# Routed experts: results scattered to two token tables and summed on the matmul engine, instead of gathered after the last unit

## The chip, the cores and the metric

The kernel runs on one core of one Trainium2 chip. The metric is device time in microseconds (us) of one execution. TensorE (PE) does matmuls into the eight PSUM banks, VectorE (DVE), ScalarE (ACT) and GpSimd (POOL) do elementwise work, SyncE (SP) issues plain DMAs, and POOL issues the indirect DMAs, whose rows are addressed by an index per partition.

## The reference

Four layers on 1024 tokens of width 256: a linear attention, a gated attention, a decay attention and a grouped attention with experts, each followed by `x = layernorm(x + layer(x))`. Only the end of the last layer matters here. A router picks two of eight experts for each token, and its two probabilities weigh the results:

```python
topv, topi = jax.lax.top_k(xt @ gate_w, 2);  probs = softmax(topv)
for e in range(8):
    h = silu(xt @ w1[e]) * (xt @ w3[e])
    out = out + w[:, e:e + 1] * (h @ w2[e])      # w: probs at the two picked experts, else 0
x = layernorm(x + h_attn + out)
```

## The kernel before

Tokens lie as 8 tiles of 128 (`NT` = 8). `layer1_experts` starts after the grouped attention. Every fp32 matrix of the experts is split in a high part (rounded to the matmul's fp32r) and a low part (the rest), and a product is three matmuls (`split_product`, L125).

**Routing.** The second half of the norm (`norm.apply`, L589 on DVE and L623 on ACT) writes `c.scratch`, PE turns it (L648) and multiplies it with the router's weights, and DVE works out for each token its two *slots*: the tokens of one expert get consecutive rows of a table in DRAM, each expert starting at a multiple of 128. `TILES` = 23 units of 128 slots always suffice, and all 23 are computed, empty ones too. `scratch_l`, the low part of `c.scratch`, is made in two halves, the first on POOL (L2103), the second on DVE (L2169).

**Getting the rows to their units.** POOL scatters each of the 8 token tiles twice (16 indirect DMAs, L2108) to `slot_rows` in DRAM, which SP had filled with zeros long before. Units 0 to 3 don't wait for this: PE gathers their rows with one-hot matmuls (L2426). When the 16 scatters have landed SP loads the rows of units 4 and 5, then the weights of expert 3, then the rows of units 6 to 9, 10 to 15 and 16 to 22 (L2079). PE turns a unit's rows (`turn`, L2434) in the order that is written out by hand; `turn(4)` is the first that needs the scatters, `turn(6)` the first that needs the second load.

**A unit.** `up` (two projections, 24 matmuls in all with their products), SiLU on ACT, `gate` on DVE, `turn_hidden` (L2459), high and low parts, `down` (12 matmuls to one half of PSUM bank 7), then DVE copies the result to `rows[:, j]` (`leave`, L2237) and SP stores it to `slot_outs`, row by row as the slots lie (L2093). `down(j)` waits until `leave(j - 1)` is done.

**Weights.** SP loads an expert's three matrices (1536 KB) to one of two stages. Experts 0 and 1 are split by ACT and DVE, experts 2 to 7 by POOL: three high parts (L2122), then three low parts (L2126), then `w_ready`. Of each ring of three experts POOL waits until the units of the expert it overwrites are done.

**The end.** POOL waits until all 23 stores have landed and gathers with 16 indirect DMAs (L2131, for each token tile the rows of its first and of its second slot). For each token tile, as it lands, DVE adds both rows with their probabilities to `c.y` (L2298, twice), takes the moments (L2301, L2304, L2306), ACT the root (L2387), DVE the reciprocal and the shift (L2308, L2309), ACT applies them (L2390) and SP stores the tile.

Of the kernel before, what the change touches and what calls it, by code (L numbers as in the profile page):

```python
# [53 lines left out]
class Core:  # L54


    def __init__(self, nc, dram, out, ctx):
# [17 lines left out]
        self.scratch = self.tile(ctx, "scratch", [P, NT, D])  # L75

        self.slot_rows = nc.dram_tensor("slot_rows", (SLOTS, D), F32).ap()
# [583 lines left out]
def layer0_gated_attention(c, norm, following, next_norm, later_norm):  # L661
# [10 lines left out]
    with ExitStack() as ctx:  # L672
# [22 lines left out]
        z_ready, picked_ps, kv_ready, nm_ready, pT_ready, rs_ready, o_scaled, chain = c.sems(  # L695
# [3 lines left out]
        c.finished += pe_sems  # L699
# [488 lines left out]
def layer1_decay_attention(c, norm, pre, following, next_norm):  # L1188
# [7 lines left out]
    with ExitStack() as ctx:  # L1196
# [24 lines left out]
        TURN_AT = PAIRS + 12  # L1221
        SECOND_AT = 1
# [52 lines left out]
        def _(dve):  # L1275
# [31 lines left out]
            for s in range(STEPS + 1):  # L1307
# [21 lines left out]
                if 6 <= s < 14:  # L1329
                    following.split(dve, s - 6)  # L1330
                if s == PAIRS + 3:
                    scale(0)
                    dve.wait_ge(acc_out, 2)
# [214 lines left out]
def layer1_grouped_attention(c, norm, pre, next_norm, router):  # L1548
# [7 lines left out]
    with ExitStack() as ctx:  # L1556
# [54 lines left out]
        def _(sp):  # L1611
# [18 lines left out]
            zeros = c.warm16[:].bitcast(F32).unsqueeze(1).broadcast_to((P, SLOTS // P, D))  # L1630
            sp.dma_start(c.slot_rows.rearrange("(n p) d -> p n d", p=P), zeros).then_inc(c.rows_zeroed, 16)
# [329 lines left out]
class RoutedExperts:  # L1961
# [4 lines left out]
    def __init__(self, c, ctx, router):  # L1966
        self.c, self.router = c, router
        self.rows, self.rows_zeroed = c.slot_rows, c.rows_zeroed
        self.outs = c.nc.dram_tensor("slot_outs", (SLOTS, D), F32).ap()
# [4 lines left out]
def layer1_experts(c, norm, pre):  # L1974
# [8 lines left out]
    GATHERS = 8  # L1983
# [3 lines left out]
    X0, T_BANK, Y_BANK = 5, 4, 7  # L1987
    with ExitStack() as ctx:
# [19 lines left out]
        slot_max = sb("slot_max", [P, NT])  # L2008
# [16 lines left out]
        rows = sb("rows", [P, TILES, D])  # L2025
# [9 lines left out]
        back = [c.xT[:].rearrange("p k (a d) -> p (k a) d", d=D), c.scratch[:]]  # L2035
# [9 lines left out]
        back_in = c.sems(ctx, "f", " ".join(f"back_in{n}" for n in range(GATHERS)))  # L2045
        scattered, outs_in, stored, hot_made = c.cleared_sems("scattered outs_in stored hot_made")
# [9 lines left out]
        def rows_landed(eng, j):  # L2056
            n = next(n for n, (first, last) in enumerate(chunks) if j < last)
            eng.wait_ge(rows_in[n], 16)
# [10 lines left out]
        def _(sp):  # L2069
            def load_weights(e):  # L2070
                if e in (2, 3):
                    sp.wait_ge(w_low, e - 1)
                if e >= 2:
                    sp.wait_ge(w_ready, e - 1)
                sp.dma_start(stage[e % 2][:], c.dram["w_experts"][e]).then_inc(stage_in[e % 2], 16)
# [24 lines left out]
        def _(pool):  # L2100
            pool.wait_ge(norm.shift_ready, norm.so["shift_ready"] + 2)
            pool.wait_ge(s_high, 1)
            pool.tensor_tensor(scratch_l[:, 0:4, :], c.scratch[:, 0:4, :], scratch_h[:, 0:4, :].bitcast(F32), ALU.subtract).then_inc(s_low, 1)  # L2103
            pool.wait_ge(pre.rows_zeroed, 16)
            pool.wait_ge(slots_ready, 1)
            for t in range(NT):
                for k in range(2):
                    pool.indirect_dma_start(pre.rows, bass.IndirectOffsetOnAxis(slots[:, k, t:t + 1].bitcast(mybir.dt.uint32), 0), c.scratch[:, t, :], None).then_inc(scattered, 16)  # L2108
            pool.wait_ge(table_ready, 1)
            for e in range(2, EXPERTS):  # L2110
# [6 lines left out]
                pool.wait_ge(w_ready, e)  # L2117
                pool.wait_ge(stage_in[e % 2], 16 * (e // 2 + 1))
                at = e % RING * WC
                for n in range(3):  # L2120
                    cols = slice(at + PARTS[n].start, at + PARTS[n].stop)
                    pool.tensor_copy(wh[:, cols], stage[e % 2][:, PARTS[n]]).then_inc(pool_high, 1)  # L2122
                for n in range(3):
                    cols = slice(at + PARTS[n].start, at + PARTS[n].stop)
                    pool.wait_ge(pool_high, 3 * (e - 2) + n + 1)
                    low = pool.tensor_tensor(wl[:, cols], stage[e % 2][:, PARTS[n]], wh[:, cols].bitcast(F32), ALU.subtract)  # L2126
                low.then_inc(w_ready, 1)
            pool.wait_ge(outs_in, 16 * TILES)
            for t in range(NT):
                for k in range(2):  # L2130
                    pool.indirect_dma_start(back[k][:, t, :], None, pre.outs, bass.IndirectOffsetOnAxis(slots[:, k, t:t + 1].bitcast(mybir.dt.uint32), 0)).then_inc(back_in[t * GATHERS // NT], 16)  # L2131

        @block.vector
        def _(dve):
# [32 lines left out]
            weight_low(0, 0)  # L2167
            dve.wait_ge(s_high, 2)
            dve.tensor_tensor(scratch_l[:, 4:NT, :], c.scratch[:, 4:NT, :], scratch_h[:, 4:NT, :].bitcast(F32), ALU.subtract).then_inc(s_low, 1)  # L2169
# [28 lines left out]
            dve.tensor_copy(slots[:], slot_f[:]).then_inc(slots_ready, 1)  # L2198
            dve.tensor_tensor(slot_max[:], slot_f[:, 0], slot_f[:, 1], ALU.max)
# [9 lines left out]
            link(dve.tensor_tensor(slot_diff[:], slot_min[:], slot_max[:], ALU.subtract))  # L2209
            link(dve.tensor_tensor(slot_in[:], from_half[:], slot_diff[:].unsqueeze(2).broadcast_to((P, NT, 2)), ALU.mult))  # L2210
            link(dve.tensor_tensor(slot_in[:], slot_in[:], slot_max[:].unsqueeze(2).broadcast_to((P, NT, 2)), ALU.add))
# [23 lines left out]
            def leave(j):  # L2235
                dve.wait_ge(y_ps, j + 1)
                dve.tensor_copy(rows[:, j, :], ps[:, Y_BANK, j % 2 * D:(j % 2 + 1) * D]).then_inc(y_out, 1)  # L2237
# [39 lines left out]
            for j in range(5, TILES):  # L2277
                gate(j)
                hidden_low(j - 1)
                if j + 2 < TILES:  # L2280
                    row_low(j + 2)
                if j >= 6:
# [5 lines left out]
            leave(TILES - 1)  # L2288

            dve.wait_ge(p_ready, 1)  # L2290
            per = NT // GATHERS
            for g in range(GATHERS):
# [335 lines left out]
```

## Time and profile before

| | |
|---|---|
| three runs | 965.43 us median (965.05 to 967.98) |
| profiled execution | 968.8 us, span of its instructions 967.0 us |
| granted TensorE clock, mean | 0.977 |
| PE busy | 894.3 us, 92% |
| DVE, POOL, ACT busy | 654.6, 455.8, 416.8 us |
| grouped attention ends, experts begin | about 789 us into the span |
| last matmul ends | 937.4 us |

The page divides the span into 40 slices. PE is at nine tenths or more in nearly all of them up to the last, in which it is at 0 and its granted clock at 0.5: nothing is multiplied from 937.4 us on. The chain of waits, which is followed back from the last instruction, shows what fills that end.

### The profile page before, as it was taken

What the parts mean: (1) busy time and instruction counts of PE and PEld (TensorE: products, weight loads), DVE (VectorE), ACT (ScalarE), POOL (GpSimd) and SP (SyncE); (2) the same over time, 40 slices, a digit from 0 to 9 for tenths busy, and PEclk for the clock granted to TensorE, in tenths of its full rate; (3) what the DMA queues carried; (4) which work ended last, traced back from release to release, by engine and by line L of the source; (5) the groups of instructions that cost most, each with busy time, mean ns of one, the idle gap of its engine ahead of it and who ended that gap; (6) DMA issues with size and microseconds to landing.
All of it is one profiled execution on the core that took longest, in us unless ns stands there. A gap on an engine that the chain in (4) does not pass through costs nothing. (4 is left out here: it accounts for less than half of the span.)

```text
span 967.0 us, 17722 instructions
## 1 busy us (share of the span) xinstructions
PE 894.3 (92%) x6526; PEld 731.5 (76%) x6536; DVE 654.6 (68%) x1154; ACT 416.8 (43%) x1002; POOL 455.8 (47%) x409
## 2 busy tenths in 40 slices
PE   9998999988999999999999879999999978899970
PEld 5566666767888888888888668888888955788860
DVE  3577678975566675576665689778888758476436
ACT  4323456643544545445455345434232444233322
POOL 2000400015667766776766255554545414888405
PEclk9999999999999999999999899999999999999995
DMA  5000200004433433333332101131000031664014
GB/s 194 1 2 2 66 1 2 2 19 122 150 110 101 124 109 105 89 105 119 104 109 62 55 12 50 45 103 40 1 2 1 1 126 37 240 242 137 28 41 124
DMA packets 53459, 72.05 MB, mean 75 GB/s; under 512 B 4992, under 2 KB 45056, under 8 KB 52224
## 3 DMA queue, kind: packets, MB, share of 16 engines
q1 hardware_dynamic: 51840, 66.72, 21.8%
q0 software_dynamic: 1536, 4.20, 1.4%
q8 instruction: 55, 0.90, 0.4%
q14 instruction: 28, 0.23, 0.1%
HBM read 61.73 MB, written 9.18 MB: 73 GB/s over the span
## 5 line engine op out<-in xcount | busy, mean ns | idle before, releaser
L1765 ACT ACTIVATE e_probs<-ps,e_neg_max 128x256 f32<-128x256 f32 (+1 forms) x128 | 52.1, 419 | 121.9 <-DVE e_neg_max L1691 121.9
L125 PE MATMUL ps<-xTl,d_wh 128*128 128x512 f32 x192 | 80.8, 421 | 2.8 <-DVE d_s_m L1281 2.8
L1281 DVE TENSOR_TENSOR d_s_m<-ps,d_decay 128x768 f32<-128x768 f32 x64 | 58.3, 952 | 34.4 <-PE ps L1443 32.1
L1644 POOL TENSOR_TENSOR e_q_T<-xT 128x512 f32<-128x512 f32 x32 | 41.1, 1284 | 82.0 <-DVE xT L1679 82.0
L1086 POOL TENSOR_TENSOR d_wh<-d_stage,d_nought 128x512 fp32r<-128x512 f32 x32 | 43.2, 1351 | 75.8 <-PE ps L125 33.1
L125 PE MATMUL ps<-xTh,d_wh 128*128 128x512 f32 x192 | 76.3, 397 | 0.0
L125 PE MATMUL ps<-xTh,d_wl 128*128 128x512 f32 x192 | 76.1, 396 | 0.0
L615 POOL TENSOR_TENSOR n_rstd<-n_var,half_power 128x4 f32<-128x4 f32 x6 | 6.1, 1023 | 133.5 <-DVE n_var L561 133.4
L1360 ACT ACTIVATE d_gated_hi<-d_gated 128x512 fp32r<-128x512 f32 x32 | 20.2, 632 | 108.6 <-DVE d_gated L1287 108.6
L125 PE MATMUL ps<-f_wl,wh_gated 128*128 (+2 forms) x184 | 65.2, 354 | 1.9 <-DVE f_rows L2237 0.7
L125 PE MATMUL ps<-f_wh,wh_gated 128*128 (+2 forms) x184 | 62.8, 341 | 0.0
L125 PE MATMUL ps<-f_wh,wl_gated 128*128 (+2 forms) x184 | 62.6, 340 | 0.0
L868 ACT ACTIVATE g_probs<-ps,g_neg_max 128x256 f32<-128x256 f32 (+1 forms) x128 | 43.2, 422 | 31.6 <-DVE g_neg_max L786 31.1
L1157 DVE TENSOR_TENSOR wl_gated<-d_q_T,wh_gated 128x512 fp32r<-128x512 f32 x32 | 22.7, 710 | 50.0 <-ACT wh_gated L1142 50.0
L1650 POOL TENSOR_TENSOR e_probs<-e_probs,e_rsum 128x256 f32<-128x256 f32 x64 | 52.5, 841 | 6.8 <-DVE e_rsum L1696 6.8
L1094 POOL TENSOR_TENSOR d_wh<-d_stage,d_nought 128x256 fp32r<-128x256 f32 x32 | 26.9, 839 | 48.2 <-PE ps L125 48.0
L1272 POOL TENSOR_TENSOR d_sq_sum<-d_sq_sum,d_sq 128x512 f32<-128x512 f32 x32 | 44.2, 1382 | 10.6 <-ACT d_sq L1364 10.6
L125 PEld LDWEIGHTS ps<-xTl,d_wh 128*128 128x128 f32 x192 | 36.4, 190 | 15.7 <-issue 8.8
L1088 POOL TENSOR_TENSOR d_wl<-d_stage,d_wh 128x512 fp32r<-128x512 f32 x32 | 43.3, 1352 | 2.5
L2126 POOL TENSOR_TENSOR f_wl<-f_stage,f_wh 128x1024 fp32r<-128x1024 f32 x18 | 43.3, 2435 | 0.0
L125 PEld LDWEIGHTS ps<-xTh,d_wh 128*128 128x128 f32 x192 | 36.4, 189 | 9.0
L125 PEld LDWEIGHTS ps<-xTh,d_wl 128*128 128x128 f32 x192 | 36.5, 190 | 7.1
(389 smaller groups left out, 2894.3 us busy)
## 6 DMA issues: line engine op xcount, KB each, us to landing
d_decay<-in_decay SPq DMA_DIRECT2D x32, 384.0 KB, 3.8
f_stage<-in_w_experts SPq DMA_DIRECT2D x8, 1536.0 KB, 7.1
d_stage<-in_w_decay SPq DMA_DIRECT2D x32, 256.0 KB, 3.0
d_stage<-in_w_decay SPq DMA_DIRECT2D x32, 128.5 KB, 3.4
d_stage_v<-in_w_decay SPq DMA_DIRECT2D x32, 128.0 KB, 2.3
d_stage<-in_w_decay SPq DMA_DIRECT2D x32, 128.0 KB, 2.4
slot_rows<-warm SPq DMA_DIRECT2D x1, 2944.0 KB, 10.5
slot_outs<-f_rows SPq DMA_DIRECT2D x23, 128.0 KB, 3.2
```

Of the source, the lines that this page charges most:

```text
L125: mm = pe.matmul(out, w(k), x(k), start=(opens and n == 0), stop=(closes and n == 3 * len(ks) - 1))
L868: ex = act.activation(probs[:, n % KEPT, i, cols], ps[:, banks(n) + i, cols], ACT.Exp, bias=neg_max[:, n % 4, t, i:i + 1])
L1086: pool.tensor_tensor(wh, qk, self.nought[:].unsqueeze(1).broadcast_to((P, KD, 2 * P)), ALU.add).then_inc(self.qk_high, 1)
L1088: pool.tensor_tensor(wl, qk, wh.bitcast(F32), ALU.subtract).then_inc(self.qk_split, 1)
L1094: pool.tensor_tensor(wh, g, self.nought[:].unsqueeze(1).broadcast_to((P, KD, P)), ALU.add).then_inc(self.g_high, 1)
L1157: dve.tensor_tensor(self.q_lo, self.q_T[:], self.q_hi.bitcast(F32), ALU.subtract).then_inc(self.qk_lo, 1)
L1272: pool.tensor_tensor(sq_sum[:, cols], sq_sum[:, cols], sq[:], ALU.add).then_inc(sq_added, 1)
L1281: dve.tensor_tensor(s_m[:, s % 2, 2 * b:2 * b + 2, :], ps[:, 2 + 2 * b:4 + 2 * b, 0:CAUSAL], decay[:], ALU.mult).then_inc(sm_ready, 1)
L1644: pool.tensor_tensor(dst, by_cos[:, n % 2, :], by_sin[:, n % 2, :], ALU.add).then_inc(roped, 1)
L1650: mul = pool.tensor_tensor(part, part, rsum[:, s % 4, t, :].unsqueeze(2).broadcast_to((P, 2, cols.stop - cols.start)), ALU.mult)
L1765: ex = act.activation(probs[:, s % KEPT, i, cols], ps[:, 2 + i, cols], ACT.Exp, bias=neg_max[:, s % 4, t, i:i + 1], accum_out=sums[:, s % ...
L2126: low = pool.tensor_tensor(wl[:, cols], stage[e % 2][:, PARTS[n]], wh[:, cols].bitcast(F32), ALU.subtract)
```

## The change

- `slot_rows` gets two columns more (1032 bytes a row): the token's number and its larger slot, scattered along with the row. The table is filled beforehand with zeros, 2048 + partition, and -1. Units 0 to 3 get these two columns by a DMA of their own, ahead of the row loads of units 6 on.
- From them DVE works out, during units 13 to 16, where each slot's result belongs: row `token` of a first table if the slot is the smaller of its token, row `1024 + token` of a second if it is the larger, and a spare row if the slot is empty.
- POOL scatters each unit's result there (`unit_out`, 23 indirect DMAs), all of them behind its last weights. The 23 plain stores of SP and the 16 gathers are gone.
- SP loads the first table (four DMAs of two token tiles) when units 0 to 21 have landed, and the second when the last has.
- PE sums in PSUM: identity times `c.y`, then diagonal matrices of the probabilities times the first and the second table, all fp32. DVE builds the 16 diagonals behind the last unit's copy. DVE and ACT read the sums from PSUM, in pairs of token tiles, with the factors of a pair behind the moments of the next.
- POOL splits an expert's up weights first (`w_ready`), its down weights last (`w_low`); `down` waits for the latter.
- The first half of `scratch_l` moves from POOL to DVE.

```diff
+        self.scratch_rows = self.tile(ctx, "scratch", [P, NT, D + 2])
+        self.scratch, self.tokens, self.slot_max = self.scratch_rows[:, :, 0:D], self.scratch_rows[:, :, D], self.scratch_rows[:, :, D + 1]
+        self.slot_rows = nc.dram_tensor("slot_rows", (SLOTS, D + 2), F32).ap()
...
+            sp.dma_start(rows[:, 0:GATHERED, D:D + 2], pre.rows[0:GATHERED * TILE, D:D + 2].rearrange("(n p) d -> p n d", p=P)).then_inc(rows_in[1], 16)
             for n in range(1, len(chunks)):
                 load_rows(n)
-            for j in range(TILES):
-                if 4 <= j < EXPERTS:
-                    load_weights(j)
-                sp.wait_ge(y_out, j + 1)
-                sp.dma_start(pre.outs[j * TILE:(j + 1) * TILE, :], rows[:, j, :]).then_inc(outs_in, 16)
+            for e in range(4, EXPERTS):
+                load_weights(e)
+            sp.wait_ge(outs_in, 16 * (TILES - 1))
+            for g in range(PAIRED):
+                load_back(0, 2 * g, 2).then_inc(first_in[g], 16)
+            sp.wait_ge(last_in, 16)
+            for g in range(PAIRED):
+                load_back(1, 2 * g, 2).then_inc(back_in[g], 16)
...
-            pool.wait_ge(norm.shift_ready, norm.so["shift_ready"] + 2)
-            pool.wait_ge(s_high, 1)
-            pool.tensor_tensor(scratch_l[:, 0:4, :], c.scratch[:, 0:4, :], scratch_h[:, 0:4, :].bitcast(F32), ALU.subtract).then_inc(s_low, 1)
...
+            def unit_out(j):
+                pool.wait_ge(dest_ready, 1)
+                pool.wait_ge(y_out, j + 1)
+                pool.indirect_dma_start(pre.outs, bass.IndirectOffsetOnAxis(dest[:, j:j + 1].bitcast(mybir.dt.uint32), 0), rows[:, j, 0:D], None).then_inc(
+                    outs_in if j < TILES - 1 else last_in, 16)
...
+                high(0)
+                high(1)
+                low(0)
+                low(1).then_inc(w_ready, 1)
+                high(2)
+                low(2).then_inc(w_low, 1)
+            for j in range(TILES):
+                unit_out(j)
...
+            for k in range(2):
+                for t in range(NT):
+                    dve.tensor_scalar(scaling[:, k, t, :], c.ident, p_of[:, k, t:t + 1], None, ALU.mult).then_inc(scaled, 1)
...
+            for g in range(PAIRED):
+                moments(g)
+                if g >= 1:
+                    factors(g - 1)
+            factors(PAIRED - 1)
...
             turn_hidden(TILES - 1)
-            down(TILES - 2, at[TILES - 2][1])
-            down(TILES - 1, at[TILES - 1][1])
+            down(TILES - 2, *at[TILES - 2])
+            for t in (2, 3):
+                added(t, c.ident, c.y[:, t, :], first=True)
+            down(TILES - 1, *at[TILES - 1])
+            for t in (0, 1, 4, 5, 6, 7):
+                added(t, c.ident, c.y[:, t, :], first=True)
+            keep_warm(c, pe, ps[:, X0, :], 12)
+            for g in range(PAIRED):
+                pe.wait_ge(scaled, 2 * g + 2)
+                pe.wait_ge(first_in[g], 16)
+                ... two matmuls, scaling[:, 0, t, :] by back[0][:, t, :]
+            for g in range(PAIRED):
+                pe.wait_ge(back_in[g], 16)
+                for t in (2 * g, 2 * g + 1):
+                    mm = added(t, scaling[:, 1, t, :], back[1][:, t, :])
+                mm.then_inc(summed, 1)
```

## Rows read from the trace of the kernel before

**Rows 1.** Chain of waits from 834 us on: start us, us, what.
```profile
834.77 2.38 DMA slot_rows<-scratch,f_slots
837.17 2.76 DMA f_rows<-slot_rows
...
935.01 0.44 DVE f_rows L2237
...
935.68 1.70 PE ps L125 x12
937.41 0.43 DVE f_rows L2237
...
939.53 0.26 issue
...
964.29 0.60 ACT x L2390
```

**Rows 2.** Groups from 937 us on: busy us, mean ns of one | idle before.
```profile
L2131 POOL DMA_INDIRECT xT<-slot_outs,f_slots x8 | 7.8, 978 | 37.5 <-DMA slot_outs<-f_rows 35.4 <-issue 2.1
L2131 POOL DMA_INDIRECT scratch<-slot_outs,f_slots x8 | 7.7, 958 | 2.4 <-issue 2.4
```

**Rows 3.** Timeline, POOL: start us, us, instruction [idle before].
```profile
808.49 1.27 POOL L2108 DMA_INDIRECT slot_rows<-scratch,f_slots  x1 [14.10 <-DVE f_slots L2198]
810.07 2.85 POOL L2108 DMA_INDIRECT slot_rows<-scratch,f_slots  x1 [0.31 <-issue]
...
897.28 7.10 POOL L2126 TENSOR_TENSOR f_wl<-f_stage,f_wh 128x1024 fp32r<-128x1024 f32 x3
```

**Rows 4.** Timeline, 960.3 to 961.9 us: moments and factors of one token tile.
```profile
960.39 0.43 DVE L2301 BATCH_NORM_STATS2 f_stats<-y 128x6 f32<-128x256 f32 x1
...
961.26 0.20 ACT L2387 ACTIVATE f_sd<-f_var 128x1 f32<-128x1 f32 x1 [1.36 <-DVE f_var L2306]
961.49 0.16 DVE L2308 RECIPROCAL f_rstd<-f_sd 128x1 f32<-128x1 f32 x1 [0.27 <-ACT f_sd L2387]
961.69 0.16 DVE L2309 SCALAR_TENSOR_TENSOR f_shift<-f_mv,f_rstd 128x1 f32<-128x1 f32 x1
```

**Rows 5.** Groups by shape: busy us, mean ns of one | idle before.
```profile
L465 PE MATMUL ps<-a_wo,a_o_nT 128*128 128x256 f32 x32 | 8.0, 392 | 0.1
L2349 ACT ACTIVATE wh_gated<-ps,r_wcol 128x256 fp32r<-128x256 f32 x4 | 1.7, 470 | 8.9 <-PE ps L2426 8.9
L591 DVE TENSOR_SCALAR scratch<-y,n_mv,n_comb 128x256 f32<-128x256 f32 x6 | 2.1, 402 | 0.0
```

**Rows 6.** Timeline, 788 to 802 us: the second half of the norm and the router.
```profile
788.92 1.41 DVE L547 BATCH_NORM_STATS2 n_stats<-y 128x6 f32<-128x256 f32 x4 [0.32 <-PEq L1556]
...
791.84 2.70 DVE L589 TENSOR_SCALAR scratch<-y,n_rstd 128x256 f32<-128x256 f32 x2
791.96 0.91 ACT L623 ACTIVATE scratch<-y,n_rstd 128x256 f32<-128x256 f32 x2 [0.53 <-DVE n_shift L583]
792.00 2.39 POOL L2103 TENSOR_TENSOR f_wl<-scratch,f_wh 128x1024 fp32r<-128x1024 f32 x1 [14.07 <-DVE n_shift L583]
...
794.59 1.10 PE L648 MATMUL ps<-consts,scratch 128*128 128x128 f32 x8 [1.80 <-DVE scratch L589]
...
798.67 1.22 DVE L2169 TENSOR_TENSOR f_wl<-scratch,f_wh 128x1024 fp32r<-128x1024 f32 x1
...
801.40 0.23 DVE L2171 COPY f_lg<-ps 128x64 f32<-128x64 f32 x1 [1.51 <-PE ps L2407]
```

**Rows 7.** Timeline, SP and PE, around the row loads (the last SP row covers three issues).
```profile
837.64 0.42 SPq L2075 DMA_DIRECT2D f_stage<-in_w_experts  x1
838.11 3.84 SPq L2079 DMA_DIRECT2D f_rows<-slot_rows  x3
...
846.22 0.38 PE L2434 MATMUL ps<-consts,f_rows 128*128 128x128 f32 x2
```

**Rows 8.** DMA issues: KB each, us from issue to landing.
```profile
f_rows<-slot_rows SPq DMA_DIRECT2D x1, 512.0 KB, 7.9
```

More of the change, by code:

```diff
@@ L1987, in layer1_experts @@
     X0, T_BANK, Y_BANK = 5, 4, 7
+    DEST_AT = 13
     with ExitStack() as ctx:
@@ L2024, in layer1_experts @@
         wl = sb("wl", [P, RING * WC], F32R)
-        rows = sb("rows", [P, TILES, D])
+        rows = sb("rows", [P, TILES, D + 2])
+        spare_picked, spare_used = picked[:].rearrange("p a t e -> p (a t e)"), used[:].rearrange("p e n -> p (e n)")
+        slot_id, second, empty, dest_f = (spare_picked[:, n * TILES:(n + 1) * TILES] for n in range(4))
+        dest = sb("dest", [P, TILES], mybir.dt.int32)
+        order = spare_used[:, 0:2 * NT].rearrange("p (a t) -> p a t", a=2)
+        shares = spare_used[:, 2 * NT:6 * NT].rearrange("p (a t) -> p a t", a=4)
+        p_of = sb("p_of", [P, 2, NT])
         rows_hot = [w[:].rearrange("p k (a s) -> p (k a) s", s=WINDOW) for w in (c.xTh, c.xTl)]
@@ L2165, in weight_low @@
                 return dve.tensor_tensor(wl[:, cols], stage[e][:, PARTS[part]], wh[:, cols].bitcast(F32), ALU.subtract)
-            weight_low(0, 0)
-            dve.wait_ge(s_high, 2)
-            dve.tensor_tensor(scratch_l[:, 4:NT, :], c.scratch[:, 4:NT, :], scratch_h[:, 4:NT, :].bitcast(F32), ALU.subtract).then_inc(s_low, 1)
+            for half in range(2):
+                four = slice(4 * half, 4 * half + 4)
+                dve.wait_ge(s_high, half + 1)
+                dve.tensor_tensor(scratch_l[:, four, :], c.scratch[:, four, :], scratch_h[:, four, :].bitcast(F32), ALU.subtract).then_inc(s_low, 1)
+                if half == 0:
+                    weight_low(0, 0)
             dve.wait_ge(lg_ps, 1)
@@ L2460, in turn_hidden, with down @@
                 mm.then_inc(hid_ps, 1)
-            def down(j, at):
+            def down(j, ready, at):
+                pe.wait_ge(w_low, ready)
                 pe.wait_ge(lo_ready, j + 1)
-                if j < 2:
-                    pe.wait_ge(w_low, j + 1)
                 need(pe, y_out, j)
@@ L2493, in _ @@
             turn(5)
-            down(3, at[3][1])
+            down(3, *at[3])
             up_next(4)
@@ L2502, in _, with added @@
                 if j >= 6:
-                    down(j - 2, at[j - 2][1])
+                    down(j - 2, *at[j - 2])
+            def added(t, factor, tile, first=False):
+                return pe.matmul(ps[:, t // 2, t % 2 * D:(t % 2 + 1) * D], factor, tile, start=first and t % 2 == 0, stop=not first, skip_group_check=True)
             turn_hidden(TILES - 1)
-            down(TILES - 2, at[TILES - 2][1])
-            down(TILES - 1, at[TILES - 1][1])
+            down(TILES - 2, *at[TILES - 2])
[8 more added lines that the diff above has]
+                pe.wait_ge(first_in[g], 16)
+                for t in (2 * g, 2 * g + 1):
+                    pe.matmul(ps[:, g, t % 2 * D:(t % 2 + 1) * D], scaling[:, 0, t, :], back[0][:, t, :], start=False, stop=False, skip_group_check=True)
+            pe.wait_ge(scaled, 2 * NT)
+            for g in range(PAIRED):
+                pe.wait_ge(back_in[g], 16)
+                for t in (2 * g, 2 * g + 1):
+                    mm = added(t, scaling[:, 1, t, :], back[1][:, t, :])
+                mm.then_inc(summed, 1)
 def build(nc, dram, out):
```

138 lines of the change are left out of this document (86 added, 52 removed).

## Prediction

> **What bounds the kernel now.** I read the slices of the page first: TensorE is full until the last slice and idle in that one. Then the chain of waits. It is one unbroken run of matmuls through units 4 to 22, so in that stretch only work on PE, or a wait that PE gets, changes the time; what DVE, ACT and POOL do beside it is free as long as they keep up. The chain leaves PE at 937.38 us and goes copy, store, POOL, load, DVE, ACT, final store [rows 1]. The last copy ends at 937.41 + 0.43 = 937.84 us and the span at 967.0: a tail of 29.2 us. The groups of that stretch name its owner: POOL's 16 gathers of 0.96 to 0.98 us with 0.30 between them, 16 x 1.27 = 20.3 us [rows 2]; each token tile's arithmetic hides under the next gather. The chain has one more place for this change: the 16 scatters ahead of `turn(4)`, whose last is issued at 834.77 us [rows 1], hang on the router, and the router on the norm at 792 us [rows 6].
>
> **The tail, new.** All from 937.84 us, terms in order.
> - POOL starts unit 22's scatter 0.26 us after its release, as its first gather does [rows 1].
> - Issue to landing of a scatter: 2.38 us [rows 1].
> - Beside that issue DVE builds 16 diagonals. Two scatters beside back-to-back DVE work took 1.27 and 2.85 us [rows 3], the gathers some 0.96 [rows 2]: +0.3 or +1.9. Bounds 0 and 1.9; I take the mean of the two, 1.1.
> - SP loads the second table; 256 KB landed in 2.76 us [rows 1]; with the wake-up 2.8. The first table is out of the way: unit 21's copy ends at 935.45, its scatter lands by 935.45 + 0.26 + 2.38 = 938.1, the four loads are in by about 942.5, and the second table isn't asked for before 940.5.
> - PE adds the first pair: two fp32 matmuls of 0.39 us [rows 5], overlapped in part: 0.7. At half clock 1.2.
> - DVE, four pairs. One tile takes 0.87 us from its statistics to ACT's root, 960.39 to 961.26, and 0.36 for reciprocal and shift [rows 4]. A second tile adds 0.33 for its statistics ((1.41 - 0.43) / 3 [rows 6]) and about 0.1 for the aggregate: 1.3 a pair. ACT's root hides under the factors of the pair before. 4 x 1.3 + 4 x 0.36 = 6.6 us. The loads, 0.4 to 0.5 us apart, don't bind it. Bound above: 7.4, the second tile unoverlapped.
> - ACT has four tiles left when the factors of the third pair come, 0.36 us before the last. From PSUM one is 0.47 us [rows 5], from SBUF 0.60, and two in a row take 0.91 rather than 1.2 [rows 1, 6]: 1.2 us past the last factors, at most 2.0.
> - Final store: 964.29 + 0.60 = 964.89 to 967.0, 2.1 us [rows 1].
>
> Sum 0.26 + 2.38 + 1.1 + 2.8 + 0.7 + 6.6 + 1.2 + 2.1 = 17.1 us, for 29.2: **12.1 us gained**, between 9.0 (1.9 for the diagonals, half clock, both upper bounds) and 13.2 (no collision).
>
> What is to be ready beside it: a diagonal is half as wide as the 0.40 us operation [rows 5], so the first eight are there by 937.84 + 3.2 = 941.0 and all by 944.3, against tables landing from about 940.9 and 944.4. The eight identity products and twelve warming matmuls fill PE while it would idle; two of the products stand in the 0.7 us that PE waits for the copy of unit 21 (935.01 to 935.68 [rows 1]), so the last `down` isn't later.
>
> **The scatters of units 0 to 21.** They stand in POOL's queue behind the last weights, which end at 897.28 + 7.10 = 904.4 us [rows 3]; the destinations are made at unit 14, before 900. 22 scatters of 1.27 us are issued by 932.3, before unit 21's result exists (935.45), so there is no backlog; the spare is 937.84 - 932.3 = 5.5 us, that is, a period of up to 1.52 us. The DVE work of a unit has an operand in PSUM, and POOL has no other work. They take the place of stores that cost nothing.
>
> **Up weights first, down weights last.** The sum of POOL's work is unchanged, `w_low` comes when `w_ready` came, and PE waits for neither in the chain before: 0. Waiting on both counts from registers: 0 to 0.5 us in all; `up` does it already without a gap.
>
> **The low part moved to DVE.** This gives something that lies far from the tail. At 792.0 us POOL's operation starts, and two DVE operations beside it take 2.70 us; PE's turning waits 1.80 us for them [rows 6]. The same shape undisturbed takes 0.40 [rows 5], and ACT's two tiles are done at 791.96 + 0.91 = 792.87. So PE starts at 792.9 for 794.59: 1.7 us earlier. The SBUF page of the Trainium skill (SBUF — State Buffer, the port pair that VectorE and GpSimd share) calls this an exclusive lock that the later instruction waits out in full; the rows agree, since the pair ends when POOL's ends. The moved operation costs DVE 1.22 us, and DVE idles 1.51 before the logits [rows 6], so it is covered, with 0.3 to spare. Bounds: 0 and 1.9; I take 1.7. The slots are released one small operation later, +0.1.
>
> By the box on VectorE blocking a GpSimd DMA on that page of the Trainium skill, descriptors can't be written while such an instruction holds the ports. The diagonals are of that kind, so by the rule the last scatter may wait for all sixteen, some 3 us, and the time would be 954 instead of 952. This bears on the 1.1 us above, whose ends are from rows.
>
> **Wider rows and the small DMA.** SP issues one DMA more, of 512 pieces of 8 bytes, ahead of the load that `turn(6)` needs. That load was issued at 838.11 and landed 7.9 us later, at 846.0 [rows 7, 8]; PE used it at 846.22 [rows 7]. So only 0.2 us is spare, and anything that the queue gets ahead of it shifts PE. One more issue takes SP some 0.47 us (837.64 to 838.11 [rows 7]). With the pieces themselves I take a stall of 0.5 us, bounds 0 and 2.
> By the Trainium skill's page DMA: Bandwidth & Descriptors (How a descriptor splits into AXI transactions), 1032-byte rows that begin at no multiple of 256 bytes cost up to 40 beats for 32, a quarter more. No row here shows such a row; by it the 768 KB of units 4 to 9, some 2 us at the rate of that stretch, take 0.5 us more, which is inside the bound.
>
> **Nearly free:** blank columns, token numbers and a broader fill of `slot_rows` during the attentions (nobody waits for the fill for 160 us; DVE gets three to five small operations where it waits for ACT), and some twelve operations of about 0.2 us in units 13 to 16, where the additions to `c.y`, which end with unit 12, leave DVE nearly 2 us a unit. The first 16 scatters: same count, same DVE work beside them, 0 to +1.
>
> **Sum.** -12.1 - 1.7 + 0.1 + 0.5 = -13.2 us against the profiled execution's own 968.8 us (span 967.0): 955.6. The median of the three runs lies 3.4 us below that execution, so I give 965.4 - 13.2 = **952.2 us**. The ends of the terms: tail -13.2 to -9.0, norm -1.9 to 0, stall 0 to 2, first scatters 0 to 1, registers 0 to 0.5.
>
> **Rivals.**
> 1. *A backlog on POOL.* The 16 scatters of before had a mean period of (834.77 - 808.49) / 15 = 1.75 us [rows 1, 3], because DVE work of SBUF alone stood beside them. With that period the 22 end at 904.4 + 38.5 = 942.9 instead of 937.84, the last scatter is 5 us late, and the time 957.3. For it: same instruction, same engine. Against: in the units DVE reads PSUM, and the 16 gathers beside the final DVE work kept 1.27. Shown by POOL having no idle time before the last scatter. 10%.
> 2. *The wider rows are late.* The rows of units 4 to 9 come 2 to 3 us later, PE stops at `turn(4)` or `turn(6)` and its clock falls after it; the norm's gain is eaten. About 955.0. For it: the 0.2 us of spare. Against: the volume grows by 0.8%. 14%.
> 3. *The norm's gain doesn't arrive* (another wait stands behind it, the stage of expert 0 or ACT's order), tail as forecast: 953.9. 10%.
> 4. *Slower: a 1032-byte row takes two descriptors.* Then each of the 16 scatters, which lie on the path to `turn(4)`, costs POOL twice its 0.96 us, +15.4 us, and PE idles as long. Time 952.2 + 15.4 = 967.6, slower by 0.2%, and with the halved clock behind the gap some 969. It decides from 13.2 / 16 = 0.83 us more per scatter. For it: these are the first rows over 1024 bytes on that queue. Against: a row is one contiguous run on both sides. 4%.
>
> **How the numbers follow.** Forecast 62%, own range 950.5 to 954.5. Rivals 2 and 3 reach to 955.5 and 1 to 957.3. Below, the smallest tail and no stall give 950.3. Range 949.8 to 957. What a measurement of this kernel can tell from no change is about 0.3%, 2.9 us. Faster by more: forecast and rivals 1 to 3, 95%; within: 2%; slower: 3%, rival 4 with its clock.
>
> **What would show it.** Right: a tail of 16 to 19 us from the last copy; L648 at about 792.9 us and L589 near 0.7 us for two; POOL idle before each of the last two or three result scatters; the last one longer than 1 us; no new gap in PE's run but at `turn(6)`. Wrong: POOL without a gap up to the last scatter (1), `turn(6)` waiting 2 us for its DMA (2), L2407 not 1.6 us earlier (3), the first scatters' shortest time near 1.9 us instead of 0.96 (4).

## The result, and the profile after

| | before | changed |
|---|---|---|
| median | 965.57 us, 20 runs (962.41 to 969.83) | 959.65 us, 20 runs (954.38 to 963.42) |
| ratio, 95% interval | | 0.9932 [0.9913, 0.9951] |
| profiled execution, its span | 968.8, 967.0 us | 961.75, 959.9 us |
| mean granted clock | 0.977 | 0.987 |

Faster by 0.7%, 6.6 us by the ratio, where 13.2 us were forecast; 952.2 us was below every one of the twenty runs, and 959.65 lies above the range that was given (949.8 to 957).

The experts' stage begins at different moments in different executions (783.3 to 790.4 us over the profiles of this case, with either kernel), so times in it are compared from its first instruction, the first `bn_stats` of the norm. I cut it in three: up to the first matmul of `turn(4)`, from there to the end of the last unit's copy, and the tail. All three columns are differences of rows like those below.

| kernel (profiled execution) | to `turn(4)` | `turn(4)` to last copy | tail | whole |
|---|---|---|---|---|
| before | 51.05 | 97.87 | 29.2 | 178.1 |
| changed | 48.52 | 104.82 | 19.3 | 172.6 |
| the changed kernel a second time, on another chip | 49.04 | 101.85 | 19.9 | 170.8 |

So the tail gave 9.9 us and the front 2.5, and the middle, for which 0.5 us was allowed, took 4.0 in one execution and 6.9 in the other. In the second profile 5.9 us of the forecast are missing: 3.5 in the middle and 2.8 in the tail, with 0.4 more than forecast in the front.

The chain of waits of the changed kernel shows all three (start us, us, what; it answers to [rows 1]):

```profile
834.47 8.89 DMA f_rows<-slot_rows
843.40 0.69 PE ps L2515 x2
...
897.49 1.86 DVE f_used L2343
...
902.99 0.44 DVE f_rows L2285
...
903.67 6.00 PE ps L128 x24
...
941.35 3.79 DMA slot_outs<-f_rows,f_dest
...
945.16 3.83 DMA scratch<-slot_outs
```

Before, the chain ran through PE alone from unit 4 to 22. Now DVE stands in it in its pass for unit 15 (called unit 15 below), with operations on 8 columns and then the copy of an earlier unit's result. The waits of PE from 826 to 936 us name the same two places (engine, line, what it waited for: us in total, times, longest):

```profile
PE ps L2515 <- DMA f_rows<-slot_rows: 4.4, 2, 2.6
PE ps L128 <- DVE f_rows L2285: 3.0, 1, 3.0
```

The timeline of DVE and POOL in the passes of units 13 to 15 shows what those operations wait for (start us, us, instruction [idle before]):

```profile
887.47 1.86 DVE L2333 TENSOR_SCALAR f_picked<-f_iota,place 128x23 f32<-128x23 f32 x1
...
889.59 0.18 DVE L2335 TENSOR_SCALAR f_picked<-f_rows 128x23 f32<-128x23 f32 x1
...
894.55 4.76 POOL L2167 TENSOR_TENSOR f_wl<-f_stage,f_wh 128x1024 fp32r<-128x1024 f32 x2
...
895.21 0.69 DVE L2275 TENSOR_TENSOR f_hid<-w_gated,ps 128x512 f32<-128x512 f32 x1 [1.25 <-PE ps L128]
...
897.41 1.93 DVE L2343 TENSOR_TENSOR f_used<-f_slot_f 128x8 f32<-128x8 f32 x1
...
899.24 1.05 POOL L2162 CAST f_wh<-f_stage 128x1024 fp32r<-128x1024 f32 x1
899.37 0.94 DVE L2344 TENSOR_TENSOR f_used<-f_slot_f 128x8 f32<-128x8 f32 x1
...
900.35 0.17 DVE L2345 TENSOR_TENSOR f_used<-f_used,f_gs 128x16 f32<-128x16 f32 x1
900.38 2.35 POOL L2167 TENSOR_TENSOR f_wl<-f_stage,f_wh 128x1024 fp32r<-128x1024 f32 x1
...
900.56 2.19 DVE L2346 TENSOR_TENSOR f_used<-f_used,f_gs 128x8 f32<-128x8 f32 x1
902.79 0.17 DVE L2347 TENSOR_TENSOR f_used<-f_used,f_gs 128x8 f32<-128x8 f32 x1
```

L2343 ends at 899.34, POOL's second L2167 at 899.31; L2344 ends at 900.31, POOL's cast at 900.29; L2346 ends at 902.75, POOL's next L2167 at 902.73. L2345 begins 0.03 us ahead of POOL's operation and takes 0.17. L2275, which reads PSUM, takes 0.69 us under the same POOL operation. So a DVE operation on SBUF alone that begins under one of POOL's waits it out, although it has only 8 columns, and five operations worth 0.9 us hold the queue from 897.41 to 902.96. Behind them, in the same pass, stands the copy `leave(13)`, for which `down(14)` waits. Its place by the rhythm is 882.63 (the last copy before these passes) + 3 x 4.84 (a unit) = 897.2; it came at 902.99, 5.8 us late. Of this 2.8 us were spare, and PE waited the other 3.0. The operations for the destinations met the same thing in unit 13: one on 23 columns took 1.86 us, and `leave(11)` came at 890.04 instead of 887.5. That stayed inside the spare, so PE lost about 0.2 us there.

The windows show the second price (us, busy time of PE, PEld, DVE, ACT, POOL, granted clock, DMA share, GB/s):

```profile
900.00:904.00 4.00, 1.00 (x9) 0.77 (x7) 3.86 (x7) 1.11 (x3) 3.67 (x3) 1.00 0.00 0
904.00:908.00 4.00, 4.00 (x18) 3.57 (x17) 1.79 (x7) 0.00 (x0) 2.89 (x3) 0.57 0.30 102
```

PE idles for 3.0 us and then has a granted clock of 0.57, that is 1.2 GHz for most of that window: 24 matmuls (12 of a `down`, 12 of an `up`) take 6.00 us instead of 4.18.

The norm and the router, which answer to [rows 6]:

```profile
787.26 1.41 DVE L550 BATCH_NORM_STATS2 n_stats<-y 128x6 f32<-128x256 f32 x4 [0.32 <-PEq L1571]
...
790.18 0.61 DVE L592 TENSOR_SCALAR scratch<-y,n_rstd 128x256 f32<-128x256 f32 x2
...
791.34 1.06 PE L651 MATMUL ps<-consts,scratch 128*128 128x128 f32 x8 [0.22 <-ACT scratch L626]
...
798.11 0.22 DVE L2219 COPY f_lg<-ps 128x64 f32<-128x64 f32 x1 [0.58 <-PE ps L2488]
```

And the end, timeline from 939 us on, which answers to [rows 2 to 4]:

```profile
940.17 0.42 DVE L2285 COPY f_rows<-ps 128x256 f32<-128x256 f32 x1 [1.92 <-PE ps L128]
940.51 3.21 DVE L2361 TENSOR_SCALAR f_stage<-consts,f_p_of 128x128 f32<-128x128 f32 x16
941.35 1.05 POOL L2145 DMA_INDIRECT slot_outs<-f_rows,f_dest  x1 [1.38 <-DVE f_rows L2285]
941.75 2.00 SPq L2120 DMA_DIRECT2D xT<-slot_outs  x4
...
945.16 1.90 SPq L2120 DMA_DIRECT2D scratch<-slot_outs  x4
...
949.12 2.18 PE L2585 MATMUL ps<-scratch,f_stage 128*128 128x256 f32 x9 [0.36 <-DMA scratch<-slot_outs]
950.26 0.76 DVE L2366 BATCH_NORM_STATS2 f_stats<-ps 128x6 f32<-128x256 f32 x2 [6.54 <-PE ps L2585]
```

### The profile page after: what moved, and what is told of

It is laid out like the page before. It is cut to its first block and busy times, and to the rows that moved or that the text cites. A ratio compares the mean times of both kernels' runs of the same rounds, so it can differ in the third digit from the quotient of the medians.

```text
span 959.9 us, 17883 instructions
## 1 busy us (share of the span) xinstructions
PE 910.1 (95%) x6596; PEld 742.1 (77%) x6596; DVE 656.6 (68%) x1163; ACT 415.5 (43%) x998; POOL 458.9 (48%) x415
## 5 line engine op out<-in xcount | busy, mean ns | idle before, releaser
L2167 POOL TENSOR_TENSOR f_wl<-f_stage,f_wh 128x1024 fp32r<-128x1024 f32 x18 | 43.0, 2404 | 0.5
L128 PEld LDWEIGHTS ps<-f_wl,wh_gated 128*128 128x128 f32 x184 | 35.6, 193 | 9.8 <-issue 5.2
```

What stands on the lines that cost most here:

```text
L128: mm = pe.matmul(out, w(k), x(k), start=(opens and n == 0), stop=(closes and n == 3 * len(ks) - 1))
L2167: return pool.tensor_tensor(wl[:, cols], stage[e % 2][:, PARTS[n]], wh[:, cols].bitcast(F32), ALU.subtract)
```

## Experiments

The theory (A in the expectations): the five operations of unit 15 cost 4 to 5 us, because they stand beside POOL's weights. The rivals for the missing 6.6 us: the small DMA and the wider rows at `turn(6)`, the tail, and a gain of the norm that doesn't arrive. Every kernel was timed on one chip with the kernel before, 4 to 12 runs against 11 to 23 of it. The table of stages has one profiled execution each.

| kernel | median us | ratio to before | to `turn(4)` | middle | tail | whole |
|---|---|---|---|---|---|---|
| e1_shares_late | 954.26 | 0.9869 [0.9846, 0.9892] | 49.59 | 97.11 | 19.7 | 166.4 |
| e2_small_last | 959.2 | 0.9914 [0.9885, 0.9943] | 49.12 | 101.73 | 18.7 | 169.6 |
| e3_low_only | 966.6 | 0.9989 [0.9968, 1.001] | 49.17 | 98.20 | 29.4 | 176.7 |
| e4_wide_rows | 968.04 | 1.0000 [0.9983, 1.0017] | 51.05 | 98.12 | 29.3 | 178.5 |
| c1_changed | 958.23 | 0.9914 [0.9884, 0.9944] | 49.04 | 101.85 | 19.9 | 170.8 |
| e5_ops_in_before | 970.72 | 1.0042 [1.0020, 1.0064] | 51.08 | 102.78 | 29.1 | 183.0 |
| e7_no_first_table | 951.96 | 0.9838 [0.9804, 0.9871] | 48.39 | 97.85 | 18.8 | 165.0 |
| e8_rows_first | 953.31 | 0.9869 [0.9839, 0.9898] | 48.72 | 95.83 | 18.8 | 163.3 |
| e8_again | 952.98 | 0.9863 [0.9834, 0.9893] | 48.28 | 95.77 | 18.7 | 162.8 |
| e1_again | 953.42 | 0.9856 [0.9838, 0.9875] | 49.38 | 97.52 | 19.0 | 165.9 |
| e9_interleaved | 954.95 | 0.9871 [0.9848, 0.9894] | 49.68 | 95.82 | 20.3 | 165.8 |
| e10_low_on_pool | 955.59 | 0.9879 [0.9858, 0.9900] | 50.33 | 97.58 | 19.0 | 166.9 |

**The shares late (e1_shares_late).** The five operations of unit 15 and the two of unit 16 that add up their results move behind POOL's last weights.

```diff
-                if j == DEST_AT + 2:
+                if j == 18:
...
-                if j == DEST_AT + 3:
+                if j == 19:
```

> The changed kernel, with the seven small operations on the probabilities (order, shares, p_of) moved from units 15 and 16 to units 18 and 19, in which POOL only issues scatters. Theory A (a DVE operation of SBUF alone waits out POOL's weight operation beside it; in the changed kernel's trace five of them, 8 or 16 columns wide, took 1.93, 0.94, 0.17, 2.19 and 0.17 us in unit 15, PE then waited 3.0 us and ran at half clock for some 2 us): each takes under 0.25 us, PE has no gap in unit 15, and the time falls by 3.5 to 5 us against the changed kernel, to about 955 us, 1.1% under the kernel before. Rival (these operations are slow for their strided operands, or because of the scatters): they take as long in units 18 and 19, and the time stays near 959.

Measured 0.9869 against 0.9914 for e2_small_last, which keeps the operations in unit 15 and ran on the same chip: 4.9 us between the medians. (The two differ in the place of a small DMA as well; the intervals overlap a little.) On another chip the same kernel gave 0.9856 [0.9838, 0.9875] (e1_again) and the changed kernel 0.9914 [0.9884, 0.9944] (c1_changed), which don't overlap. The timeline of DVE and of POOL in unit 18:

```profile
908.91 0.15 DVE L2343 TENSOR_TENSOR f_used<-f_slot_f 128x8 f32<-128x8 f32 x1
...
909.71 0.17 DVE L2347 TENSOR_TENSOR f_used<-f_used,f_gs 128x8 f32<-128x8 f32 x1
```

```profile
908.84 0.96 POOL L2145 DMA_INDIRECT slot_outs<-f_rows,f_dest  x1 [0.30 <-issue]
```

The same five take 0.15 to 0.18 us each beside POOL's scatter, and the scatter keeps its 0.96. PE has no gap in these units. The middle falls from 101.9 to 97.1 us, and to 97.5 in e1_again. The two additions of unit 16 had taken 0.16 and 0.17 us where they stood, so the gain belongs to the five. With the next experiment, which puts them into the kernel before, this cause is shown.

**The operations alone, in the kernel before (e5_ops_in_before).** Nothing reads what they write.

```diff
+                if j == 15:
+                    dve.wait_ge(p_ready, 1)
+                    link(dve.tensor_tensor(order[:, 0], slot_f[:, 0], slot_f[:, 1], ALU.is_lt))
...
+                    link(dve.tensor_tensor(shares[:, 3], order[:, 0], p2, ALU.mult))
```

> The kernel before, with the five small operations on the probabilities put into unit 15 as the changed kernel has them, and nothing else; their result is not used. Theory A (they wait out POOL's weight operations of expert 7 one after the other): three of the five take 0.9 to 2.4 us each, PE gets a gap of 2 to 3 us in unit 15 and half clock behind it, and the kernel is 3 to 5 us slower than before. Rival (only the changed kernel's order of POOL's work, or its destination operations ahead of them, makes the gap): under 1 us slower.

Slower by 0.42%, 4.1 us (1.9 to 6.2), with the middle 4.9 us longer than in the kernel before. Timeline, unit 15:

```profile
893.50 7.05 POOL L2129 TENSOR_TENSOR f_wl<-f_stage,f_wh 128x1024 fp32r<-128x1024 f32 x3
...
895.95 2.32 DVE L2288 TENSOR_TENSOR f_used<-f_slot_f 128x8 f32<-128x8 f32 x1
...
901.69 0.38 PE L125 MATMUL ps<-f_wl,wh_gated 128*128 x1 [3.08 <-DVE f_rows L2240]
```

Here three of the five took 0.59, 2.32 and 2.27 us under POOL's operation. Taken out of the changed kernel the five give 4 to 6 us by the ratios and 4.2 to 4.7 in the middle; put into the kernel before they cost 4: both directions agree.

**The small DMA behind the row loads (e2_small_last).**

```diff
-            sp.dma_start(rows[:, 0:GATHERED, D:D + 2], ...).then_inc(rows_in[1], 16)
             for n in range(1, len(chunks)):
                 load_rows(n)
+            sp.dma_start(rows[:, 0:GATHERED, D:D + 2], ...).then_inc(rows_in[3], 16)
```

> The changed kernel, with the DMA of the two extra columns of units 0 to 3 (512 pieces of 8 bytes) issued behind all row loads instead of ahead of them. Theory B (it delays the load that turn(6) needs): that load lands 0.5 us or more sooner after its issue than the 8.9 us of the changed kernel, PE's wait at turn(6) falls from 2.6 to 2 us or less, the time by 0.5 to 1.5 us. Rival (the wider rows, or the weights ahead of them, make the load late): the wait stays at 2.4 to 2.7 us and the time within 0.3 us.

959.2 us, not to be told from the changed kernel (0.9914 against 0.9932, and c1_changed 0.9914). The rows for `turn(6)` landed 8.0 us after their issue and PE didn't wait there; in the changed kernel's two executions they took 8.9 and 7.7 us, and PE waited 2.63 and not at all. So one execution's 2.6 us at `turn(6)`, which I first took for a cost of the small DMA, mostly varies from execution to execution; the timed runs give the DMA's place no price.

The profiles show what it goes with. Between `turn(4)` and `turn(6)` PE has 24 matmuls. Where the clock stayed up behind `turn(4)` they took 4.3 us, and PE then waited for the rows: 2.63 us in the changed kernel, 1.76 in e7 and 1.49 in e10. Where it had fallen they took 5.2 us, and there was no wait or nearly none (c1, e1, e2; 0.2 us in e1_again). So the rows come at their own time, and a fast PE stands there waiting for them.

**The wider rows alone (e4_wide_rows),** 1032 bytes instead of 1024 in the kernel before, the two columns zero.

```diff
-        self.slot_rows = nc.dram_tensor("slot_rows", (SLOTS, D), F32).ap()
+        self.slot_rows = nc.dram_tensor("slot_rows", (SLOTS, D + 2), F32).ap()
...
-                    pool.indirect_dma_start(pre.rows, ..., c.scratch[:, t, :], None)
+                    pool.indirect_dma_start(pre.rows, ..., c.scratch_rows[:, t, :], None)
```

> The kernel before, with 258 columns instead of 256 in the slot table, in the scattered rows and in the row loads (the two extra columns hold zeros and are not used). Theory C (1032-byte rows cost nothing to scatter and little to load): the shortest scatter issue stays 0.96 us, the four row loads land within 0.5 us of the kernel before's 2.8, 7.9, 9.7 and 11.8 us, time within 0.1%. Rival (they are late): the load for turn(6) lands 0.7 us or more later and PE waits there; 1 to 3 us more.

Nothing: 1.0000, within 1.6 us either way. The issues show it (KB, us to landing): 7.9 as in [rows 8]. By an estimate from the splitting that the Trainium skill describes (DMA: Bandwidth & Descriptors, How a descriptor splits into AXI transactions) such rows would take up to a quarter more; the landings don't agree.

```profile
f_rows<-slot_rows SPq DMA_DIRECT2D x1, 516.0 KB, 7.9
f_rows<-slot_rows SPq DMA_DIRECT2D x1, 258.0 KB, 2.8
```

**The low part alone (e3_low_only),** moved to DVE in the kernel before.

```diff
-            pool.tensor_tensor(scratch_l[:, 0:4, :], c.scratch[:, 0:4, :], scratch_h[:, 0:4, :].bitcast(F32), ALU.subtract)...
...
+            for half in range(2):
+                four = slice(4 * half, 4 * half + 4)
+                dve.wait_ge(s_high, half + 1)
+                dve.tensor_tensor(scratch_l[:, four, :], c.scratch[:, four, :], ..., ALU.subtract).then_inc(s_low, 1)
```

> The kernel before, with the first half of the low part of the experts' input moved from POOL to DVE and nothing else. Theory: the two DVE operations of the norm take 0.7 us instead of 2.7, the router's logits come 1.6 us earlier, as in the changed kernel; the gain carries through to the end if PE isn't held elsewhere: 1 to 2 us, 0.1 to 0.2%. Rival (the scatters set turn(4), and turn(6) hangs on its load): the logits come 1.6 us earlier, yet the time falls by under 0.7 us.

Timed inconclusive: 0.9989, -3.1 to +1.0 us. In its profile the two scaling operations take 0.61 us and PE begins 4.08 us into the stage instead of 5.67:

```profile
791.88 0.61 DVE L589 TENSOR_SCALAR scratch<-y,n_rstd 128x256 f32<-128x256 f32 x2
...
793.05 1.07 PE L648 MATMUL ps<-consts,scratch 128*128 128x128 f32 x8 [0.20 <-ACT scratch L623]
```

`turn(4)` comes 1.9 us earlier and the whole stage is 1.4 us shorter.

**The changed kernel again (c1_changed),** no edit, on the chip of e5, e7 and e8.

> The changed kernel itself, so that it stands beside the others on one chip. Both theories: 0.7% under the kernel before, five operations of up to 2.2 us in unit 15 and a gap of some 3 us in PE there.

The gap of 3.0 us in unit 15 is there again, with the same durations; the wait at `turn(6)` is not.

**The low part back on POOL (e10_low_on_pool),** in the version with the late shares.

```diff
+            pool.wait_ge(s_high, 1)
+            pool.tensor_tensor(scratch_l[:, 0:4, :], c.scratch[:, 0:4, :], scratch_h[:, 0:4, :].bitcast(F32), ALU.subtract).then_inc(s_low, 1)
```

> The late shares with the first half of the low part back on POOL, beside the two scaling operations of DVE. If the low part's move gives what it did in the changed kernel's trace: the two scaling operations take 2.7 us again instead of 0.6, PE's turning starts about 1.6 us later, and the time is 1 to 2 us above e1_again. Rival (the wait for the scatters at turn(4) and the clock behind it swallow it, as the run of the low part alone suggests): less than 0.5 us.

Timeline of its norm:

```profile
793.33 2.54 DVE L592 TENSOR_SCALAR scratch<-y,n_rstd 128x256 f32<-128x256 f32 x2
...
793.49 2.23 POOL L2137 TENSOR_TENSOR f_wl<-scratch,f_wh 128x1024 fp32r<-128x1024 f32 x1 [14.06 <-DVE n_shift L586]
```

PE begins at 5.50 us of the stage again (4.09 in e1_again), `turn(4)` 0.95 us later, the whole is 1.0 us longer. The medians lie 2.2 us apart in the expected direction, but the intervals overlap. PE's start moves by 1.4 to 1.6 us in every comparison (e3, e10, the changed kernel), near the forecast 1.7. At `turn(4)` the gain is 1.9 us in e3, 0.95 in e10 and 2.0 to 2.5 in the changed kernel. No timed comparison by itself shows it.

**Nearly no first table (e7_no_first_table).** On e1, the four loads of the first table fetch 2 of 256 columns, which leaves most of its share of the sum out of the output.

```diff
+                if k == 0:
+                    return sp.dma_start(back[k][:, t:t + n, 0:2], source[:, :, 0:2])
```

> The kernel of e1_shares_late (the probabilities' operations in units 18 and 19), with the four loads of the first token table cut from 256 columns to 2 each, so that the first table's part of the sum is left out. In e1 the last scatter took 3.95 us from issue to landing and the second table's first load 3.96. Theory D (both share the DMA engines with the megabyte of the first table): the scatter lands in 2.4 to 2.8 us and the load in 2.8 to 3.1, and the time falls by 2 to 2.6 us. Rival (the scatter is slow for its 128 separate target rows, the load for reading what has just been written): both stay within 0.3 us, time within 0.5 us.

The last scatter, 3.8 us in the changed kernel and 3.95 in e1, lands 2.8 us after its issue (934.10 to 936.9). In the nine profiles that load both tables it is 3.8 to 4.2. But the tail, 18.8 us, is only 0.9 and 0.3 us shorter than in e1's two profiles, because PE bounds it (chain, start us, us, what):

```profile
932.88 2.59 PE ps L2587 x12
...
935.52 2.54 PE ps L142 x11
938.06 3.45 PE ps L2601 x16
941.51 0.88 PE ps L2587 x4
```

Identity products, eleven of the warming matmuls and the first table's products stand back to back. The traffic beside the scatter does lengthen it, by 1.0 to 1.4 us; behind it stands PE. The same three pieces, 8.6 us from the last `down` on, are the chain also in e2, e1_again, both profiles of e8 and e10, so in eight of the nine profiles with both tables the work on PE and the transfers end within 1 us of each other (e9, below, has another order). The timed runs, 0.9838 against 0.9869 and 0.9856 of the late shares, overlap; the 2 us or more that were expected are not there.

**The rows before the weights (e8_rows_first, e8_again).** On e1, the load of the rows of units 6 to 9 goes ahead of expert 3's weights, the small DMA behind them.

```diff
+            load_rows(1)
             load_weights(3)
-            sp.dma_start(rows[:, 0:GATHERED, D:D + 2], ...).then_inc(rows_in[1], 16)
-            for n in range(1, len(chunks)):
+            sp.dma_start(rows[:, 0:GATHERED, D:D + 2], ...).then_inc(rows_in[2], 16)
+            for n in range(2, len(chunks)):
```

> The kernel of e1_shares_late, with the load of the rows of units 6 to 9 issued ahead of the weights of expert 3, and the small DMA behind those weights. Theory B2 (turn(6) waits because 1536 KB of weights stand ahead of its rows): the rows land within 5 us of their issue, PE's wait at turn(6) and the half clock behind it go, and the time falls by 2 to 4 us against e1. Rival (the weights of expert 3, 1.5 us later, hold POOL and then `up` of a unit): the wait moves there, and less than 1 us is gained.

> The late shares with the rows of units 6 to 9 loaded ahead of expert 3's weights, measured beside the late shares alone on one chip. Theory (the clock that falls behind the wait at turn(4) or turn(6) is paid for by the late rows): 1 to 3 us below e1_again, since the earlier profile waited 2.1 us at turn(4) with the clock at 1.0 behind it, where the late shares alone waited 3.1 us with the clock at 0.64. Rival (turn(4) waits for the scatters in any case, and the wait there is what costs): within 0.8 us of it.

> The late shares alone, as the comparison for the other three kernels on this chip: ratio to the kernel before 0.987, as it was (0.9846 to 0.9892), 953 to 955 us.

The rows landed 4.3 us after issue instead of about 8, PE didn't wait at `turn(6)`, and the clock stayed up behind `turn(4)`: in both profiles the middle is 1.3 to 1.8 us and the whole stage 2.6 to 3.6 us shorter than in e1's two. Not all of that is the edit's. The front, which it doesn't touch, makes 0.7 to 1.3 us of it, and the clock stayed up behind `turn(4)` also in three profiles without the edit (the changed kernel, e7, e10). What the edit does there is that PE, when it is fast, no longer waits for the rows. The timed runs don't show a gain: 0.9863 against 0.9856 on one chip, 952.98 against 953.42 us. The runs of either spread over 5 to 9 us, so a gain up to 2 or 3 us is neither shown nor excluded.

**The tables interleaved (e9_interleaved).** On e8: two loads of the first table, then alternately one of each behind the last scatter; PE sums in that order, with 6 warming matmuls for 12.

```diff
+                if g == 1:
+                    sp.wait_ge(last_in, 16)
+                    load_back(1, 0, 2).then_inc(back_in[0], 16)
+                if 2 <= g and g - 1 < PAIRED:
+                    load_back(1, 2 * (g - 1), 2).then_inc(back_in[g - 1], 16)
...
+            for k, g in ((0, 0), (0, 1), (1, 0), (0, 2), (1, 1), (0, 3), (1, 2), (1, 3)):
+                table(k, g)
```

> The previous version (late shares, rows first) with the two tables' loads interleaved, so that only four token tiles of the first table lie ahead of the last scatter, and PE sums in that order. Theory (the last scatter and the second table's load are long, 3.8 and 3.8 us, because the first table's 1 MB flows beside them): the last scatter lands in about 2.8 us as without the first table, the first pair of the second table in about 3, and the time is 1.5 to 2.5 us below e8_again. Rival (what is taken from in front comes back behind: the pairs now come 1.8 us apart on PE and in the queue, more than DVE's 1.4 a pair): first pair earlier, last pair not, less than 0.7 us either way.

The forecast gain isn't there. Its chain:

```profile
929.60 4.02 DMA slot_outs<-f_rows,f_dest
...
934.54 4.43 DMA scratch<-slot_outs
...
940.22 0.86 PE ps L2607 x4
```

The scatter takes 4.02 us with 512 KB of loads beside it, as it does beside 1 MB. The first load of the second table did come in 2.7 us, as forecast, but the next took 4.43 with the first table's beside it: PE sums the first pair 0.4 us earlier after the last copy than in e8_again, and the last pair 2 us later. That is the rival, at a higher price than it named. The tail is 20.3 us for e8's 18.8, and the time no better (0.9871 against 0.9863).

## Why the prediction was wrong

The step that failed is the one headed **Nearly free**: "some twelve operations of about 0.2 us in units 13 to 16, where the additions to `c.y`, which end with unit 12, leave DVE nearly 2 us a unit". Their cost by themselves was right, their number nearly (fourteen), and so was DVE's spare time. But they got no neighbour: POOL splits the last experts' weights in just those units, in operations of 2.35 us ([rows 3]: 7.10 for three). [Rows 6] already showed what that does, and the same prediction used it for the norm, under **The low part moved to DVE**: two DVE operations of SBUF took 2.70 us beside POOL's 2.39. Carried over, each operation that begins under one of POOL's waits for its end, up to 2.4 us, instead of the planned 0.2. Measured, the five held DVE for 5.55 us, which made `leave(13)` 5.8 us late, with 2.8 of spare, and left a gap of 3.0 in PE and 1.8 of half clock behind it. The runs put 4 to 5 us in that place, most of the 6.6 that are missing.

Of the rest, by steps:

- *The tail, 17.1 us.* Measured 19.3 in the changed kernel and 18.7 to 19.9 in seven other profiles of it and its variants, e7 and e9 aside. The terms: POOL's start 0.75 for 0.26 (also 0.76 in e7, so it belongs to this scatter); scatter to landing 3.79 for 2.38 + 1.1, nearly right in sum and wrong in cause: the diagonals lengthened the issue only from 0.96 to 1.05 us, and the rest was the first table's traffic, which e7 took away. Load and wake-up 3.98 for 2.8, the largest miss, by the same traffic: the first load of the second table took 3.8 us from issue to landing here and 2.7 in e7. First pair on PE 1.14 for 0.7, since a product of 256 columns is two matmul instructions. DVE 5.50 for 6.6, which hid a part of the misses; ACT 1.96 for 1.2, store 2.2 for 2.1. Together +2.2. "The first table is out of the way" failed by its own dates: its four loads land while the last scatter flies. A term is missing beside it. The identity products and the warming were said to "fill PE while it would idle", and neither they nor the first table's products got a time. In e7's chain they take 2.6 + 2.5 + 3.5 = 8.6 us in a row from the last `down` on, that is to 8.2 us after the last copy, where the forecast has PE begin the second table after 6.5. So PE waited only 0.36 us for the second table's first load, and with faster transfers the tail would still not have come below about 18.7 us. The lower end of the tail's gain is also mis-summed: the four bounds give 9.2 us and not 9.0. The diagonals were ready sooner than its 6.4 us: all sixteen in 3.21.
- *The scatters of units 0 to 21.* Right: POOL was idle 1.4 us or more before each of the last ones. Rival 1 is out.
- *The low part.* Right as a mechanism and in size where it can be seen: 0.61 us for two, PE 1.6 us earlier in the stage. Rival 3 is not supported.
- *`turn(6)`, 0.5 us, bounds 0 to 2.* 2.6 us and 3 us more of middle in the profiled execution, none in the second. Neither the width (e4) nor the DMA's place (e2) has a measurable price. Rival 2 named the place, not the cause: the wait is there where PE's clock stays up behind `turn(4)`.
- *Rival 4, two descriptors a row.* Out: the shortest scatter of 1032-byte rows took 0.96 us, as before.
- *The diagonals beside the last scatter.* They lengthened its issue by 0.09 us. The rule cited there from the Trainium skill (SBUF — State Buffer, the box on VectorE blocking a GpSimd DMA), by which it might wait for all sixteen, isn't what the trace shows for operations of 0.20 us.

The clock was mentioned for rivals only. In a chain of PE alone a gap can cost more than its length: in unit 15 another 1.8 us behind 3.0.

The best measured versions are the late shares, with or without the rows first: 953 to 954 us, 1.3% to 1.4% below the kernel before and 0.5% to 0.7% below the changed one. Fewer warming matmuls were tried only together with the interleaved tables. By e8_again's profile they would give little alone: the first load of the second table was waited for until 938.9, and PE's work ahead of it ended at 939.26. What makes the stage begin up to 7 us earlier or later from one execution to the next is also open; between the two profiles of the late shares it is 3.2 us, where their spans differ by 2.7.

## To carry to other kernels

Price an added operation together with what its neighbour engine does at that moment, not by its size: here a DVE operation on SBUF alone that began under POOL's elementwise work cost what was left of POOL's, and even eight columns took 2 us. Put such operations where POOL only issues DMAs or idles, or give them an operand in PSUM. When a stage is shortened, list again what flies beside its new critical transfer, and check that the filler work isn't itself the next bound.

## What the runs showed of the hardware

- DVE's `tensor_tensor` on 8 columns with both inputs in SBUF took 1.93, 0.94 and 2.19 us beside POOL's elementwise operations and ended 0.02 to 0.03 us after them; the same with POOL issuing a scatter took 0.15 to 0.18 (e1), and one on 16 columns that began 0.03 us ahead of POOL's operation took 0.17. A `tensor_scalar` on 23 columns took 1.86 and 0.18. The Trainium skill (SBUF — State Buffer, Who interferes with whom) says that two SBUF inputs contend with a POOL operation that reads SBUF, and that the later one waits in full; the trace agrees.
- For a DMA that POOL issues, the diagonals did nearly no harm and another operation much: sixteen back-to-back `tensor_scalar` operations on SBUF left the last scatter at 1.05 us for 0.96, while a scatter among the first sixteen that began 0.14 us ahead of DVE's `tensor_tensor` with two SBUF inputs took 3.31 us (3.31 to 3.32 in the kernel before, c1, e1, e7 and e8 too). That the one holds up the other is read from their overlap; no run took it away. The timeline of the changed kernel:

```profile
813.18 3.31 POOL L2139 DMA_INDIRECT slot_rows<-scratch,f_slots  x1 [0.31 <-issue]
...
813.32 2.34 DVE L2297 TENSOR_TENSOR xTl<-f_iota,f_slot_in 128x1024 fp32r<-128x1024 f32 x2
```

- After a wait of PE at `turn(4)` the granted clock fell in some executions and not in others, and the length did not decide it: 2.44 us in c1_changed was followed by 0.75 in the next window, 3.16 us in e9_interleaved by 1.00 throughout. Where it stayed up, and the rows were loaded behind the weights, PE waited for the next rows (above, under e2).
- 1 MB of plain loads beside it took a scatter's landing from 2.8 us (e7) to 3.8 to 4.2, and half of that volume (e9) to 4.02.
